# ScalarE's order inside an attention unit: payload rows ahead of the second exponentials, input normalising in two parts

## The chip, the cores and the metric

The kernel runs on one core of one Trainium2 chip. The metric is the device time of one execution in microseconds. The kernel before took 1568.78 us, the median of three runs (1564.93 to 1570.09).

The core's engines run side by side and meet only at semaphores: TensorE (PE in the profile, its weight loads PEld), VectorE (DVE), ScalarE (ACT), GpSimd (POOL) and SyncE (SP, which only issues DMAs here). Each engine works its own list of instructions strictly in the order in which it is written, so a wait at the head of a list holds everything behind it.

## The reference, cut to what matters

`x` is [64, 128, 256], the context `ctx` is [64, 128, 192], and a mask hides some context keys.

```
lat  = layernorm(layernorm(x));  xn = layernorm(ctx) * g + b         # per token
q    = lat @ Wq;  k, v = [xn @ Wkv ; lat @ Wlkv]                     # 4 heads of 64, 256 keys
attn = softmax(rmsnorm(q) * rmsnorm(k) * scale, masked)
x    = x + (attn @ v) @ Wo + bo
n    = layernorm(x)
s    = sigmoid(n @ router) + bias;  best 2 of 4 groups, best 4 of 32 experts, weights w
x    = x + sum_k w_k * expert_k(n) + shared_expert(n)
```

All of it is computed in fp32. The first part, up to the choice of experts, is called the attention stage here. Only that stage is touched by the change.

## The kernel before, in words

**Units.** The 64 batches are worked in 32 units of two batches (j = 0 and 1). A token is a partition, so one batch is one tile of 128 rows. Each engine has a loop `in_order(step, UNITS)`; its `step(s)` handles several units at once: `s` is the unit whose attention is computed, `a = s + 1` is the unit whose queries, keys and values are projected, `s + 2` is the unit whose inputs are normalised and turned, `cc = s - 1` is the unit whose finished rows are normalised again and copied for the experts, and `r = s - 2` is the unit whose rows are ranked and given a place in the experts' lists. Order inside a step is written out by hand for every engine.

**Names and lines that matter below.**

- PE, in its own order: `scores(s,0)` (L676, L680), `project_q`, `project_kv`, `project_v` of `a` (L620, L631/L632, L645), `turn_probs(s,0)` (L689), `project_q(a,1)`, `scores(s,1)`, `project_kv(a,1)`, `mix_values(s,0)` (L701), `turn_probs(s,1)`, `turn_o(s,0)` (L710), `project_v(a,1)`, `turn_k(a,0)` (L657/L658), `mix_values(s,1)` (L701), `positions(r)` (L739 to L743), `turn_n1(cc)` (L607), `out_proj(s,0)` (L719), `turn_o(s,1)` (L710), `turn_k(a,1)`, `logits(cc)` (L728), `turn_q(a)` (L665), `out_proj(s,1)`, `turn_inputs(s+2)` (L590 to L597).
- ACT: `exps` (L996) needs `maxima` of DVE; `projected_kv` (L978, L979, L981) needs `project_kv`; `probs_copy` (L1005) needs `turn_probs`; `o_copy` (L1012) needs `turn_o`; `values_copy` (L988) needs `project_v`; `k_copy` (L1028) needs `turn_k`; `n1_copy` (L1017) needs `turn_n1`. `rows_to_scatter(cc, j)` (L952, one instruction that writes 128x1024 from 128x256) needs DVE's `norms` of this step and an old payload buffer that is free. `normalise(s+2)` needs the same `norms`; it makes `x_hat` (L938, two instructions) and counts `xhat`, then `c_hat` (L943, two instructions) and counts `hats`.
- DVE: `maxima(s,0)` (L1282), the statistics and `norms(s+2)` (ends with L1271), `scale_first(a)` (L1276), `maxima(s,1)` (L1282), `top_scores` and `best_groups` of `r`, `normalise_o(s,0)` (L1290, L1292), `best_experts` and `choose_experts` of `r` (L1344 to L1366; L1362 writes `chosen`), `square_sums(a,1)` (L1242), `scale_second(a)` (nine short links and L1311, which multiplies 128x768 in place), `normalise_o(s,1)` (L1290, L1292), `read_ranks(r)`, `residual(s,0)` (L1302), `assign(r)`, `residual(s,1)`.
- POOL: `add_bias(s+2)` (L507, 128x512 added in place, waits for `hats`), then `places`, `mask_bias(s+2)` (L499, L501), `weights` and the eight indirect DMAs of `scatter(s-2)` (L548), some of which wait for steps of PE so that they are spread over time.
- SP: the loads of a later unit and the blank list pages; a load waits for `hats` and for `mask_ready`, which `mask_bias` counts.

**Waits that tie them.** `mix_values(s,1)` waits for `pt_ev` (both copies of `probs_copy(s,1)`) and for `ot_ev` (`o_copy(s,0)`), because it writes where `turn_o(s,0)` wrote. `turn_n1(cc)` waits for both rows of `rows_to_scatter(cc)`. `turn_o(s,1)` waits for `on_done`, the end of `normalise_o(s,1)`, and in DVE's list that stands behind `scale_second(a)`:

```
pe.wait_ge(pt_ev, b + 1)
pe.wait_ge(pc_free, b + 1)
ge(pe, ot_ev, b)
```

Of the kernel before, what the change touches and what calls it, by code (L numbers as in the profile page):

```python
# [54 lines left out]
def ge(eng, sem, value):  # L55

    if value > 0:
        eng.wait_ge(sem, value)
# [6 lines left out]
def at(start, n):  # L65
    return slice(start, start + n) if isinstance(start, int) else bass.ds(start, n)
# [21 lines left out]
def build(nc, x, ctx, mask, ln_x_g, ln_x_b, ln_l_g, ln_l_b, qn_g, kn_g, wq, wkv, wlkv, wo, bo,  # L88
# [7 lines left out]
    with ExitStack() as c:  # L96
# [203 lines left out]
        def paid(u):  # L300

            if u.n == UNITS - 1:
                return pay_last
            return pay_mid if u.n % 3 == 1 else pay[:, 0:2] if u.n % 3 == 0 else pay[:, 2:4]
# [5 lines left out]
        def scattered(b, units):  # L310

            return 16 * 2 * TOPK * len(range(b, units, 3))
# [618 lines left out]
        def _(act):  # L931
            act.wait_ge(made, MADE)

            def normalise(u):
                act.wait_ge(dN, N_LINKS * (u.n + 1))
                ge(act, t_x, u.n)
                for j in range(2):
                    a = act.activation(x_hat[:, j, :], x1[:, at(2 * u.n + j, 1), :].rearrange("p a n -> p (a n)"),  # L938
                                       ACT.Identity, bias=nb[:, j:j + 1], scale=ra[:, j:j + 1])
                a.then_inc(xhat, 1)  # L940
                ge(act, t_c, u.n)
                for j in range(2):
                    a = act.activation(c_hat[:, j, :], c_in[:, u.par, j, :],  # L943
                                       ACT.Identity, bias=nb[:, 2 + j:3 + j], scale=ra[:, 2 + j:3 + j])
                a.then_inc(hats, 1)

            def rows_to_scatter(u, j):
                if j == 0:
                    act.wait_ge(dN, N_LINKS * (u.n + 4))
                    if u.n != UNITS - 1:  # L950
                        ge(act, scat[u.n % 3], scattered(u.n % 3, u.n))
                act.activation(paid(u)[:, j, :, 0:D], x1[:, at(2 * u.n + j, 1), :].to_broadcast([P, TOPK, D]),  # L952
                               ACT.Identity, bias=nb[:, 4 + j:5 + j], scale=ra[:, 4 + j:5 + j]).then_inc(pay_x, 1)

            def inputs(u):
                act.wait_ge(t_x, u.n + 1)
                ge(act, pc_full, 2 * u.n)
                for k in range(2):
                    a = act.activation(lnT[:, k, :], ps[0][:, k * D:(k + 1) * D], ACT.Identity,  # L959
                                       bias=bl[:, k:k + 1], scale=gl[:, k:k + 1])  # L960
                a.then_inc(e_x, 1)
                act.wait_ge(t_c, u.n + 1)
                act.activation(cT[:, 0, :], ps[1][:, 0:D], ACT.Identity, bias=bx[:, 0:1], scale=gx[:, 0:1])
                act.activation(cT[0:KC, 1, :], ps[1][0:KC, D:2 * D], ACT.Identity,
                               bias=bx[0:KC, 1:2], scale=gx[0:KC, 1:2]).then_inc(e_c, 1)

            def projected_q(u, j):
                b = 2 * u.n + j
                act.wait_ge(pa_full, b + 1)
                ge(act, ss_done, b - 1)  # L970
                act.activation(sq[:, j, 0:2 * D], ps[2][:, :], ACT.Square)
                ge(act, t_q, u.n)
                act.activation(raw[:, j, 0:2 * D], ps[2][:, :], ACT.Copy).then_inc(pa_free, 1)

            def projected_kv(u, j):
                b = 2 * u.n + j
                act.wait_ge(pb_full, b + 1)
                act.activation(sq[:, j, 2 * D:3 * D], ps[3][:, 0:D], ACT.Square).then_inc(sq_full, 1)  # L978
                act.activation(raw[:, j, 2 * D:3 * D], ps[3][:, 0:D], ACT.Copy)  # L979
                ge(act, pv_full, 2 * u.n - 3 + j)  # L980
                act.activation(vv[:, 4 * u.par + 2 * j, :, 0:DH],  # L981
                               ps[3][:, D:2 * D].rearrange("p (h d) -> p h d", d=DH), ACT.Copy).then_inc(pb_free, 1)

            def values_copy(u, j):

                b = 2 * u.n + j
                act.wait_ge(pc_full, b + 1)
                act.activation(vv[:, 4 * u.par + 2 * j + 1, :, 0:DH],  # L988
                               ps[4][:, 0:D].rearrange("p (h d) -> p h d", d=DH), ACT.Copy).then_inc(pc_free, 1)

            def exps(u, j):
                b = 2 * u.n + j
                act.wait_ge(m_done, b + 1)
                ge(act, pt_full, b - 1)
                for g in range(H):
                    a = act.activation(probs[:, j, g, :], psS[:, g // 2, g % 2], ACT.Exp,  # L996
                                       bias=nmax[:, j, g:g + 1])
                a.then_inc(exp_done, 1)

            def probs_copy(u, j):  # L1000
                b = 2 * u.n + j
                act.wait_ge(pt_full, b + 1)
                ge(act, pv_full, b - 1)
                for key in range(2):
                    a = act.activation(probsT[:, j, key, :], psS[:, key].rearrange("p a n -> p (a n)"), ACT.Copy)  # L1005
                a.then_inc(pt_ev, 1)

            def o_copy(u, j):
                b = 2 * u.n + j
                act.wait_ge(ot_full, b + 1)  # L1010
                ge(act, y_full, b)
                act.activation(oT, psO[:, 0:D], ACT.Copy).then_inc(ot_ev, 1)  # L1012

            def n1_copy(u):
                act.wait_ge(t_n, u.n + 1)
                ge(act, lg_full, u.n)
                act.activation(n1T.rearrange("p k n -> p (k n)"), ps[0][:, :], ACT.Copy).then_inc(e_n, 1)  # L1017

            def logit_exp(u):
                act.wait_ge(lg_full, u.n + 1)  # L1020
                ge(act, ch_done, u.n)
                act.activation(esc[:, :, :].rearrange("p j e -> p (j e)"), ps[4][:, D:D + 2 * E], ACT.Exp,
                               scale=-1.0).then_inc(lg_exp, 1)

            def k_copy(u, j):
                act.wait_ge(t_k, 2 * u.n + j + 1)
                ge(act, s_full, 2 * (u.n - 2) + j + 1)
                act.activation(kT[:, 2 * u.par + j].rearrange("p k n -> p (k n)"), ps[1 - j][:, :], ACT.Copy)\  # L1028
                   .then_inc(e_k, 1)

            def q_copy(u):

                act.wait_ge(t_q, u.n + 1)
                act.activation(qT[:, u.par].rearrange("p k j n -> p (k j n)"), ps[1][:, :], ACT.Copy,
                               scale=gqk[:, 0:1]).then_inc(e_q, 1)

            def step(s):
                a, cc = s + 1, s + -1
                if s.exists():
                    exps(s, 0)  # L1040
                if a.exists():
                    projected_q(a, 0)
                    projected_kv(a, 0)
                    values_copy(a, 0)
                if s.exists():
                    probs_copy(s, 0)
                if a.exists():
                    projected_q(a, 1)
                if s.exists():
                    exps(s, 1)  # L1050
                if (s + 2).exists():
                    normalise(s + 2)
                if cc.exists():
                    rows_to_scatter(cc, 0)
                if a.exists():
                    projected_kv(a, 1)
                if s.exists():
                    probs_copy(s, 1)
                    o_copy(s, 0)
                if a.exists():  # L1060
                    values_copy(a, 1)
                if cc.exists():
                    rows_to_scatter(cc, 1)
                if a.exists():
                    k_copy(a, 0)
                if cc.exists():
                    n1_copy(cc)
                if s.exists():
                    o_copy(s, 1)
                if a.exists():  # L1070
                    k_copy(a, 1)
                if cc.exists():
                    logit_exp(cc)
                if a.exists():
                    q_copy(a)
                if (s + 2).exists():
                    inputs(s + 2)

            normalise(Unit(0, 0))
            act.wait_ge(consts, 16 * CONSTS)  # L1080
            inputs(Unit(0, 0))
            for j in range(2):
                projected_q(Unit(0, 0), j)
                projected_kv(Unit(0, 0), j)
                values_copy(Unit(0, 0), j)
            normalise(Unit(0, 1))
            k_copy(Unit(0, 0), 0)
            k_copy(Unit(0, 0), 1)
            act.wait_ge(gains, 2)
# [524 lines left out]
```

## Time and profile before

| | us |
|---|---|
| median of the runs | 1568.78 |
| the profiled execution | 1573.22 |
| its span, first to last instruction | 1571.3 |
| PE busy | 1474.5 (94%) |
| DVE busy | 1131.4 (72%) |
| ACT busy | 992.0 (63%) |
| POOL busy | 642.6 (41%) |

Busy shares are means over the whole program. The attention stage runs from about 30 us to about 890 us; in it DVE is busy more than eight tenths and PE more than nine. A `PE` row and its duration can overlap the next one, since matmuls are pipelined; what shows a stall is the bracket at the end of a row, which gives the idle time before it and the instruction whose end released it. The granted clock of TensorE stands in the columns PEclk: 1.00 is 2.4 GHz and 0.50 is 1.2 GHz. All rows that are read below are of the profiled execution, so sums are made against 1573.22 us.

### The profile page before, as it was taken

How to read it: one execution, taken by the hardware profiler on the slowest of the kernel's cores; microseconds unless marked ns; L12 is line 12 of the kernel's file. 1: busy time of each engine (PE TensorE's matmuls, PEld its weight loads, DVE VectorE, ACT ScalarE, POOL GpSimd, SP SyncE). 2: the span in 40 equal slices, each digit the busy share in tenths (PEclk: the TensorE clock that was granted, in tenths of full speed). 3: DMA queues.
4: the chain of work that ended last, by engine and by line, in shares of the span. 5: the costliest groups of instructions: out<-in, count | busy, mean ns of one | idle time of the engine just before them, and what ended most of it. 6: DMA issues, size and time to landing. Idle time of an engine off the chain costs nothing.

```text
span 1571.3 us, 33151 instructions
## 1 busy us (share of the span) xinstructions
PE 1474.5 (94%) x8902; PEld 1160.9 (74%) x8902; DVE 1131.4 (72%) x4813; ACT 992.0 (63%) x2340; POOL 642.6 (41%) x760
## 2 busy tenths in 40 slices
PE   5999999999999999999999898999999999999997
PEld 2565666666566666656566676999999999997886
DVE  3568888888889888888888774555555555555878
ACT  3666767676677767676676452666666666664332
POOL 2014334343434434343433342666666666661000
PEclk9999999999999999999999799999999999999999
DMA  7122222223222222223240175555555555536886
GB/s 243 40 78 84 106 86 86 108 87 107 87 99 93 95 97 87 105 91 109 84 157 35 49 241 202 167 174 170 175 170 174 171 172 173 164 95 246 295 300 230
DMA packets 118146, 217.28 MB, mean 138 GB/s; under 512 B 19595, under 2 KB 82445, under 8 KB 116688
## 3 DMA queue, kind: packets, MB, share of 16 engines
q1 hardware_dynamic: 91856, 147.75, 29.1%
q0 software_dynamic: 26112, 67.42, 12.2%
q8 instruction: 79, 1.29, 0.3%
q14 instruction: 99, 0.81, 0.2%
HBM read 101.28 MB, written 118.00 MB: 140 GB/s over the span
## 4 chain that ended last, share of the span: by engine, by line
PE 76%; ACT 10%; DVE 8%; issue 5%; SPq 1%; DMA 0%; ACTq 0%; DVEq 0%
PE ps L882 16%; PE psS L892 8%; PE ps L620 8%; PE ps L817 6%; PE psO L701 5%; PE ps L719 4%; PE psS L680 4%; PE ps L873 4%; DVE nmax L1282 2%; PE ps L632 2%; PE psS L676 2%; PE ps L645 2%; ACT arena L996 2%; PE psS L689 2%; PE ps L631 2%
## 5 line engine op out<-in xcount | busy, mean ns | idle before, releaser
L572 POOL DMA_INDIRECT expert_out<-pay,dest x288 | 283.5, 984 | 183.8 <-issue 140.6
L1532 DVE TENSOR_TENSOR history<-history,ps 128x128 f32<-128x128 f32 x288 | 83.0, 288 | 208.1 <-ACT history L1158 208.1
L548 POOL DMA_INDIRECT lists<-pay,slot x168 | 173.6, 1034 | 127.0 <-PE psO L701 53.2
L701 PEld LDWEIGHTS psO<-arena 128*128 128x128 f32 x1024 | 131.7, 208 | 75.4 <-ACT arena L1005 51.2
L701 PE MATMUL psO<-arena 128*128 128x65 f32 x1024 | 140.8, 295 | 44.5 <-ACT arena L1012 44.5
L892 PE MATMUL psS<-arena,history 128*128 x576 | 172.1, 381 | 0.4 <-DVE history L1532 0.4
L996 ACT ACTIVATE arena<-psS,nmax 128x256 f32<-128x256 f32 x256 | 100.4, 475 | 108.2 <-DVE nmax L1282 108.2
L1158 ACT ACTIVATE history<-ps 128x128 f32<-128x128 f32 x288 | 79.9, 278 | 136.5 <-PE ps L882 136.5
L882 PEld LDWEIGHTS ps<-pad 128*128 128x128 f32 x1152 | 151.2, 191 | 9.4 <-ACT pad L1147 2.0
L882 PEld LDWEIGHTS ps<-pad,hist_j 128*128 128x128 f32 x1152 | 151.2, 192 | 7.3
L882 PE MATMUL ps<-pad 128*128 128x128 f32 x1152 | 151.9, 275 | 1.8 <-ACT pad L1152 1.8
L882 PE MATMUL ps<-pad,hist_j 128*128 128x128 f32 x1152 | 151.8, 275 | 0.0
L1539 DVE TENSOR_SCALAR pay<-psS,dest 128x256 f32<-128x256 f32 x288 | 139.4, 484 | 1.4 <-DVE dest L1545 0.8
L620 PE MATMUL ps<-arena 128*128 128x512 f32 x256 | 126.8, 619 | 0.3 <-ACT arena L959 0.3
L548 POOL DMA_INDIRECT lists<-arena,slot x88 | 91.0, 1034 | 62.5 <-PE psO L701 25.3
L1147 ACT ACTIVATE pad<-ps 128x256 f32<-128x256 f32 x288 | 108.0, 375 | 6.0 <-PE ps L873 6.0
L873 PE MATMUL ps<-ident,pay 128*128 128x128 f32 x576 | 109.8, 273 | 0.7 <-issue 0.7
L1282 DVE TENSOR_REDUCE nmax<-psS 128x4 f32<-128x1024 f32 x64 | 78.4, 1225 | 40.3 <-PE psS L680 35.0
L1152 ACT ACTIVATE pad<-arena 128x512 f32 x144 | 89.6, 622 | 0.0
L1152 ACT ACTIVATE hist_j<-arena 128x512 f32 x144 | 89.5, 622 | 0.0
L522 POOL TENSOR_TENSOR pay<-w,wsum 128x8 f32<-128x8 f32 x21 | 4.4, 210 | 205.2 <-DVE arena L1410 205.2
L892 PEld LDWEIGHTS psS<-arena,history 128*128 128x128 f32 x576 | 87.0, 191 | 0.7 <-issue 0.7
(214 smaller groups left out, 3392.0 us busy)
## 6 DMA issues: line engine op xcount, KB each, us to landing
lists<-pad SPq DMA_DIRECT2D x72, 516.0 KB, 4.3
pay<-lists SPq DMA_DIRECT2D x288, 129.0 KB
arena<-expert_out SPq DMA_DIRECT2D x32, 1024.0 KB, 6.8
x<-in_x SPq DMA_DIRECT2D x32, 256.0 KB
out<-arena SPq DMA_DIRECT2D x32, 256.0 KB, 5.7
arena<-in_ctx SPq DMA_DIRECT2D x32, 192.0 KB
expert_out<-pay,dest POOLq DMA_INDIRECT x288
arena<-in_gate SPq DMA_DIRECT2D x2, 2048.0 KB, 16.7
```

Source lines behind the costliest of these rows:

```text
L548: pool.indirect_dma_start(lists, bass.IndirectOffsetOnAxis(ap=slots(u)[:, j, k:k + 1], axis=0), paid(u)[:, j, k, :], None).then_inc(scat[u ...
L572: pool.indirect_dma_start(expert_out, bass.IndirectOffsetOnAxis(ap=dest[:, t % DESTS, 1:2], axis=0), yy[n], None, bounds_check=T * TOPK - ...
L620: m = pe.matmul(ps[2][:, :], lnT[:, k, tok], w_lat[:, k, 0:2 * D], start=k == 0, stop=k == 1)
L701: m = pe.matmul(psO[:, g * (DH + 1):(g + 1) * (DH + 1)], probsT[:, j, key, g * P:(g + 1) * P], vv[:, 4 * u.par + 2 * j + key, h, :], start ...
L873: m = pe.transpose(ps[n % 2][:, k * P:(k + 1) * P], xs[n][:, k * P:(k + 1) * P], ident[:, :])
L882: m = pe.matmul(ps[2 + n % 2][:, which * P:(which + 1) * P], w_now[n % 2][:, k, which * I:(which + 1) * I], xsT[:, n % 2, k * P:(k + 1) * ...
L892: pe.matmul(dbank[n % 2][:, 0:D], hh[:, n % 4, :], w_dn[:, at(e, 1), :].rearrange("p a n -> p (a n)"), start=True, stop=True)\
L996: a = act.activation(probs[:, j, g, :], psS[:, g // 2, g % 2], ACT.Exp, bias=nmax[:, j, g:g + 1])
L1147: act.activation(xsT[:, n % 2, :], ps[n % 2][:, 0:D], ACT.Copy).then_inc(xst_ev, 1)
L1152: act.activation(w_now[n % 2], w_gu[:, at(e, 1)].rearrange("p a k n -> p (a k) n"), ACT.Copy)\
L1282: dve.tensor_reduce(nmax[:, j, :], psS[:, :, :, :].rearrange("p r k n -> p (r k) n"), AX, ALU.max, negate=True).then_inc(m_done, 1)
L1539: dve.tensor_scalar(yy[n], dbank[n % 2][:, 0:D], dest[:, t % DESTS, 0:1].bitcast(fp32), None, ALU.mult)\
```

## The change

`normalise` becomes `normalise_x` (waits for `norms`, makes `x_hat`, counts `xhat`) and `normalise_c` (makes `c_hat`, counts `hats`). In ACT's `step(s)` the order changes; no instruction is added, removed or altered, and no other engine's list is touched.

```
 step, before                      step, after
 ...                               ...
 projected_q(a, 1)                 projected_q(a, 1)
 exps(s, 1)                        rows_to_scatter(cc, 0)
 normalise(s + 2)                  exps(s, 1)
 rows_to_scatter(cc, 0)            projected_kv(a, 1)
 projected_kv(a, 1)                normalise_x(s + 2)
 probs_copy(s, 1)                  probs_copy(s, 1)
 o_copy(s, 0)                      o_copy(s, 0)
 values_copy(a, 1)                 values_copy(a, 1)
 rows_to_scatter(cc, 1)            k_copy(a, 0)
 k_copy(a, 0)                      rows_to_scatter(cc, 1)
                                   normalise_c(s + 2)
 n1_copy(cc)                       n1_copy(cc)
 ...                               ...
```

```diff
-            def normalise(u):
+            def normalise_x(u):
                 act.wait_ge(dN, N_LINKS * (u.n + 1))
                 ge(act, t_x, u.n)
...
                 a.then_inc(xhat, 1)
+
+            def normalise_c(u):
                 ge(act, t_c, u.n)
...
                 if a.exists():
                     projected_q(a, 1)
-                if s.exists():
-                    exps(s, 1)
-                if (s + 2).exists():
-                    normalise(s + 2)
                 if cc.exists():
                     rows_to_scatter(cc, 0)
+                if s.exists():
+                    exps(s, 1)
                 if a.exists():
                     projected_kv(a, 1)
+                if (s + 2).exists():
+                    normalise_x(s + 2)
                 if s.exists():
                     probs_copy(s, 1)
                     o_copy(s, 0)
                 if a.exists():
                     values_copy(a, 1)
+                    k_copy(a, 0)
                 if cc.exists():
                     rows_to_scatter(cc, 1)
-                if a.exists():
-                    k_copy(a, 0)
+                if (s + 2).exists():
+                    normalise_c(s + 2)
```

Ahead of the loop both parts are called one after the other, as `normalise` was.

## Rows read from the trace of the kernel before

**Rows 1.** Windows view of the middle of attention: busy us (instructions) per engine, PEclk, DMA

```profile
82.35:849.54 767.19, 725.65 (x3970) 494.50 (x3971) 655.48 (x3179) 530.39 (x1150) 301.71 (x383) 0.94 0.27 96
```

**Rows 2.** Waits of PE, 82 to 850 us: total us, times, longest

```profile
PE psO L701 <- ACT arena L1012: 43.0, 29, 1.5
```

**Rows 3.** Timeline of PE, end of two units: start, us, work [idle before <-releaser]

```profile
467.16 1.97 PE L701 MATMUL psO<-arena 128*128 128x65 f32 x16 [1.49 <-ACT arena L1012]
...
489.08 1.04 PE L689 MATMUL psS<-ident,arena 128*128 128x128 f32 x8
...
491.51 0.27 PE L658 MATMUL ps<-ident,arena 128*128 128x128 f32 x1
493.26 1.97 PE L701 MATMUL psO<-arena 128*128 128x65 f32 x16 [1.48 <-ACT arena L1012]
...
495.69 1.03 PE L719 MATMUL ps<-arena 128*128 128x256 f32 x4
496.75 0.44 PE L710 MATMUL psO<-ident,arena 128*128 128x128 f32 x2
```

**Rows 4.** Timeline of ACT in the same unit

```profile
486.51 1.57 ACT L996 ACTIVATE arena<-psS,nmax 128x256 f32<-128x256 f32 x4 [1.78 <-DVE nmax L1282]
487.95 1.10 ACT L938 ACTIVATE arena<-x,nb,ra 128x256 f32<-128x256 f32 x2
488.94 0.98 ACT L943 ACTIVATE arena<-arena,nb,ra 128x192 f32<-128x192 f32 x2
489.82 1.24 ACT L952 ACTIVATE pay<-x,nb,ra 128x1024 f32<-128x1024 f32 x1
490.95 0.38 ACT L978 ACTIVATE arena<-ps 128x256 f32<-128x256 f32 x1
...
491.74 1.10 ACT L1005 ACTIVATE arena<-psS 128x512 f32<-128x512 f32 x2
492.70 0.42 ACT L1012 ACTIVATE arena<-psO 128x256 f32<-128x256 f32 x1
```

**Rows 5.** Timeline of DVE in the same unit

```profile
483.45 0.16 DVE L1271 SCALAR_TENSOR_TENSOR nb<-mv,ra 128x6 f32<-128x6 f32 x1
...
485.25 1.23 DVE L1282 TENSOR_REDUCE nmax<-psS 128x4 f32<-128x1024 f32 x1 [0.65 <-PE psS L680]
...
491.01 0.87 DVE L1362 TENSOR_TENSOR chosen<-r,t 128x64 bf16<-128x64 f32 x1
...
495.18 0.96 DVE L1311 TENSOR_TENSOR arena<-arena,rq 128x768 f32<-128x768 f32 x1
```

**Rows 6.** Timeline of PE, a unit with the clock falling behind it

```profile
438.05 2.74 PE L701 MATMUL psO<-arena 128*128 128x65 f32 x16 [1.48 <-ACT arena L1012]
```

**Rows 7.** Windows view, PE alone: busy us (instructions), PEclk, DMA share, GB/s

```profile
439.10:445.80 6.70, 6.70 (x35) 0.50 0.62 229
...
878.60:882.00 3.40, 3.40 (x24) 1.00 0.00 0
```

**Rows 8.** Timeline of DVE in unit 30, where `s + 2` doesn't exist

```profile
867.65 1.22 DVE L1282 TENSOR_REDUCE nmax<-psS 128x4 f32<-128x1024 f32 x1 [0.50 <-PE psS L680]
...
876.94 0.96 DVE L1311 TENSOR_TENSOR arena<-arena,rq 128x768 f32<-128x768 f32 x1
```

**Rows 9.** Timeline of PE in unit 30

```profile
878.51 0.44 PE L710 MATMUL psO<-ident,arena 128*128 128x128 f32 x2 [0.98 <-DVE arena L1292]
```

**Rows 10.** Timeline of POOL: the bias addition in three places

```profile
32.61 1.96 POOL L507 TENSOR_TENSOR x<-x,bo_b 128x512 f32<-128x512 f32 x1 [12.01 <-ACT arena L943]
...
55.66 1.28 POOL L507 TENSOR_TENSOR x<-x,bo_b 128x512 f32<-128x512 f32 x1 [21.09 <-ACT arena L943]
...
490.50 1.28 POOL L507 TENSOR_TENSOR x<-x,bo_b 128x512 f32<-128x512 f32 x1
```

**Rows 11.** Timeline of ACT and DVE beside the first two of them

```profile
32.49 0.96 DVE L1311 TENSOR_TENSOR arena<-arena,rq 128x768 f32<-128x768 f32 x1
...
54.59 0.99 ACT L943 ACTIVATE arena<-arena,nb,ra 128x192 f32<-128x192 f32 x2
```

More of the change, by code:

```diff
@@ L1048, in step @@
                     projected_q(a, 1)
+                if cc.exists():
+                    rows_to_scatter(cc, 0)
                 if s.exists():
                     exps(s, 1)
-                if (s + 2).exists():
-                    normalise(s + 2)
-                if cc.exists():
-                    rows_to_scatter(cc, 0)
                 if a.exists():
                     projected_kv(a, 1)
+                if (s + 2).exists():
+                    normalise_x(s + 2)
                 if s.exists():
@@ L1077, in step @@
                     inputs(s + 2)
-            normalise(Unit(0, 0))
+            normalise_x(Unit(0, 0))
+            normalise_c(Unit(0, 0))
             act.wait_ge(consts, 16 * CONSTS)
@@ L1085, in _ @@
                 values_copy(Unit(0, 0), j)
-            normalise(Unit(0, 1))
+            normalise_x(Unit(0, 1))
+            normalise_c(Unit(0, 1))
             k_copy(Unit(0, 0), 0)
```

## The prediction, made before the changed kernel ran

> **What bounds the kernel now.** I read the 40 slices first: attention fills more than half of the span, and behind the first slice PE is busy for nine tenths or eight, DVE is close behind, and ACT has room. So ACT's order matters only where ACT is the last to release PE. The view of waits says where that is: PE waits in one place, the second `mix_values` (L701), 29 times, 43.0 us in all, each time released by `o_copy` (L1012) [rows 2]. The timeline of PE shows the place: `turn_k(a,0)` ends at 491.51 + 0.27 = 491.78, and the mixing starts at 493.26 after 1.48 us of nothing [rows 3]. The timeline of ACT says why: between the second exponentials (486.51) and `probs_copy` (491.74) stand 1.87 us of normalising (487.95 to 489.82), 1.13 us of payload rows (489.82 to 490.95) and 0.79 us of projected copies [rows 4]. ACT had stood still for 1.78 us just ahead of those exponentials.
>
> The stall has a second price. From 82.35 to 849.54 us there are 28 unit periods (29 stalls) in 767.19 us: 27.40 us each, at a mean granted clock of 0.94 [rows 1]. But the period from 467.16 to 493.26, in which the clock stayed full, took 26.10 us [rows 3]. So 767.19 - 28 x 26.10 = 36.4 us are spent on a lower clock; a stretch of it is seen right behind the stall that ended at 438.05: 0.50, that is 1.2 instead of 2.4 GHz, from 439.10 to 445.80 [rows 6, 7].
>
> **The change, part by part.** Times are those of the unit that ends with the row at 496.75.
>
> *First payload rows ahead of the exponentials.* They need `norms`, which ends with L1271 at 483.45 + 0.16 = 483.61 [rows 5], and ACT, free at 486.51 - 1.78 = 484.73 [rows 4]. They end at 484.73 + 1.24 = 485.97, 0.54 us ahead of the exponentials' release. DVE always makes `norms` before `maxima(s,1)`, so the new wait can't hold the exponentials. Cost nothing, cover 1.78 us; without the cover it would be at most 1.24 us per unit.
>
> *Projected copies, then `normalise_x`.* The copies start at 487.95 instead of 490.95 and end after 0.79 at 488.74; `normalise_x` (0.99, 487.95 to 488.94) ends at 489.73 [rows 4]. `probs_copy` then waits for `turn_probs`, 489.08 + 1.04 = 490.12 [rows 3]: 0.39 us to spare.
>
> *`probs_copy` and `o_copy`.* Started at 490.15, `probs_copy` gives way to `o_copy` after 0.96, at 491.11, which ends after 0.42 at 491.53 [rows 4]. That is ahead of 491.78. The mixing follows `turn_k` directly, at about 491.62 by the spacing of 0.11 between such rows. The 1.48 us go.
>
> *Second rows and `normalise_c` behind `k_copy`.* `k_copy` can start at 491.82 and holds ACT for some 0.48 (half of `probs_copy`'s 0.96); the rows start at 492.30 and end at 493.54. `turn_n1` needs them after the mixing and `positions`, at about 493.6: even, within 0.1 us, and what follows covers that. `normalise_c` runs from 493.43 to 494.42. `hats` is then 494.42 instead of 489.92: 4.5 us late. `norms` and `turn_inputs` want it in the next unit or at the end of this one, over 5 us later: nothing. `add_bias` on POOL moves from 490.50 to 494.50 (it started 0.08 after `hats` at 55.66, against 54.59 + 0.99 [rows 10, 11]), and behind it `places`, `mask_bias` and, through `mask_ready`, SP's loads and blank pages. SP's list holds only loads and pages for later units; scatter of this unit waits for `assign` anyway. I take 0 for these; the nearest bound is the 4.0 us shift itself, against a need more than a unit away.
>
> *What is late next: DVE.* `turn_o(s,1)` started at 496.75, a moment behind the L719 rows at 495.69 [rows 3]. With PE 1.64 us earlier (493.26 to 491.62) it would be ready at about 495.1, but it waits for `normalise_o(s,1)`, behind `scale_second` on DVE. Unit 30 of this same trace shows the new arrangement, since it has no `s + 2` and so no normalising: no stall at the mixing, and 0.98 us of idleness at `turn_o`, released by DVE [rows 9]. From `maxima(s,1)` to L1311 it is 876.94 - 867.65 = 9.29 us there [rows 8], against 495.18 - 485.25 = 9.93 now [rows 5]. The 0.64 us are those that L1362 loses: it starts at 491.01 and ends at 491.88, just behind the bias addition on POOL, 490.50 + 1.28 = 491.78 [rows 5, 10]. That addition moves away from it. So on a full clock the period becomes 26.10 - 0.64 = 25.46 us, not 26.10 - 1.48.
>
> *Clock.* Behind the 0.98 us of unit 30 the clock stayed at 1.00 [rows 7], where behind 1.48 us it fell in most units. I take it that the 36.4 us come back whole; the other bound is that none do.
>
> **Sum.** 29 x 0.64 = 18.6, and 36.4: 55 us. Against the profiled execution, 1573.2 - 55 = 1518.2 us. The median of the runs is 4.4 us below that execution; since part of that spread may be the clock's, which would be gone, I take off half: **1516 us**.
>
> **Rivals.**
>
> *A. POOL takes DVE's operand.* One mechanism, and it decides the sign. The bias addition would start at 494.50; L1311, which reads two operands from SBUF, at 485.25 + 9.29 = 494.54. The trace has both orders of such a pair: L1362 waited out POOL's addition; and at 32.61 the addition took 1.96 instead of 1.28 us because L1311 had begun at 32.49 [rows 10, 11]. If POOL is first, L1311 goes on only at 494.50 + 1.28 = 495.78 and ends 0.10 + 0.96 - 0.12 later, 496.62, against 494.54 + 0.96 = 495.50: 1.12 us late (with 0.12 of its 0.96 done before it needs the operand, as L1362's rows suggest). It lies on the path to `turn_o`. The period is 25.46 + 1.12 = 26.58, PE's idleness there 0.98 + 1.12 = 2.10 us, longer than 1.48, and the clock falls after it: at 36.4 / 28 = 1.30 us a unit the period is 27.88 against 27.40, +14 us, **1587 us** on the profile's time. With falls in half the units it is 27.23, -5 us: 1568, no change. It decides at which of the two starts first, and 0.04 us is less than my chain is sure of. For it: every start is tied to PE, so the race repeats alike in each unit. Against it: each 0.05 us that ACT is later than I have it gives DVE the race, where POOL's wait costs nothing.
>
> The Trainium skill has the rule behind this race ("SBUF — State Buffer", section "Who interferes with whom"): a VectorE instruction with two SBUF inputs contends with a GpSimd instruction that reads SBUF, and whichever issues first keeps the shared pair for its whole length. This case's rows agree in both orders. By that rule the change is worth what the race gives: 1518 or 1587.
>
> *B. The race is mixed*, unit by unit. Half the units at 25.46 and half at 26.58 plus 1.30: mean 26.67, so 29 x 0.73 = 21 us: 1552 us; with fewer falls 1535. Middle 1544.
>
> *C. The clock still falls behind 0.98 us.* Then only 29 x 0.64 = 18.6 us come: 1555 us. Unit 30 speaks against it, but it is one unit.
>
> *D. The edit moves no release*, because ACT isn't what PE waits for. The view of waits names L1012 29 times, and unit 30 loses the stall with the normalising; I give it next to nothing.
>
> **How the numbers follow.** Forecast (DVE first, clock full) 0.42; A 0.26, of which 0.16 slower and 0.10 near the time before (a part of that a little faster); B 0.20; C 0.12. A measurement of this kernel can tell 0.3%, 4.7 us. Faster: 0.42 + 0.20 + 0.12 + 0.02 = 0.76; the same 0.08; slower 0.16. The range starts at 1507 (all of the 4.4 us off, and some 7 us if the unstalled units also lose their 0.1 us gaps) and goes up through C, B and the near half of A to 1574, leaving out the slower 0.16.
>
> **What the profile after would show.** Right: L1012 is gone from PE's waits at L701; L710 waits for L1292, about 0.98 us, 29 times; L952 stands ahead of L996, whose idle time falls from 1.78 to about 0.54; L1362 takes a quarter of its 0.87 us; L1311 starts 9.29 us after L1282; periods near 25.46 and a granted clock near 1.00. Wrong by A: L1311 takes about 2.1 us beside L507, L710 waits 2 us, PEclk stays near 0.94. Wrong by C: the same waits as the forecast, but PEclk at 0.94. A wait of L607 for L952 would say that the second rows come too late, one of L996 for `norms` that the first do.

## The result, and the profile after

The changed kernel takes **1624.97 us** (median of 4 runs, 1608.89 to 1627.14) where the kernel before took 1568.59 on the same chip (1564.93 to 1570.09): a ratio of 1.034 (95% interval 1.027 to 1.041). It is slower, outside the range of 1507 to 1574 us, and it went the way of rival A. The profiled execution took 1622.99 us, its span 1621.1 against 1571.3, so 49.8 us are to be found. Ratios below are of fast runs; one run, the 1661.06 us of experiment 2, was a slow one and counts only in that experiment's median. The lines of POOL and PE keep their numbers; those of ACT and DVE move by 2 to 5 (L952 becomes L954, L996 L998, L1012 L1014, L1282 L1287, L1292 L1297, L1311 L1316, L1362 L1367).

First the page of the kernel after: its engines, and the granted clock in 40 slices.

```profile
PE 1508.6 (93%) x8902; PEld 1183.9 (73%) x8902; DVE 1139.7 (70%) x4813; ACT 995.7 (61%) x2340; POOL 661.4 (41%) x760
...
PEclk9999899888988998989989989999999999999999
```

The windows view of the stretch of [rows 1], with the same columns:

```profile
82.35:849.54 767.19, 713.68 (x3714) 486.07 (x3714) 622.05 (x2991) 497.57 (x1070) 298.45 (x359) 0.90 0.25 89
```

Less work of every engine fits into the same 767.19 us, and the clock is 0.90 where it was 0.94. The waits of PE from 82 to 905 us are one row, to be laid beside [rows 2]:

```profile
PE psO L710 <- DVE arena L1297: 57.6, 28, 2.1
```

The wait for `o_copy` is gone, and a longer one, for DVE, stands in its place. The timeline of PE shows a unit and the next one's end, as [rows 3] and [rows 9] do:

```profile
485.42 0.27 PE L658 MATMUL ps<-ident,arena 128*128 128x128 f32 x1
485.58 1.97 PE L701 MATMUL psO<-arena 128*128 128x65 f32 x16
...
488.01 1.03 PE L719 MATMUL ps<-arena 128*128 128x256 f32 x4
491.10 0.49 PE L710 MATMUL psO<-ident,arena 128*128 128x128 f32 x2 [2.06 <-DVE arena L1297]
...
520.96 0.44 PE L710 MATMUL psO<-ident,arena 128*128 128x128 f32 x2 [2.06 <-DVE arena L1297]
```

The second mixing follows `turn_k(a,0)` at once; `turn_o(s,1)` comes 2.06 us late, and this period took 520.96 - 491.10 = 29.86 us. Behind it the clock is at 1.2 GHz (windows view, PE alone):

```profile
491.40:498.10 6.70, 6.70 (x30) 0.50 0.60 226
```

Why DVE is late shows in its timeline and POOL's, the pair that rival A set against each other [rows 5, 10]:

```profile
488.45 2.04 DVE L1316 TENSOR_TENSOR arena<-arena,rq 128x768 f32<-128x768 f32 x1
490.41 0.17 DVE L1295 RECIPROCAL rden<-psO 128x4 f32<-128x4 f32 x1
490.62 0.42 DVE L1297 TENSOR_TENSOR arena<-psO,rden 128x256 f32<-128x256 f32 x1
```

```profile
488.42 1.26 POOL L507 TENSOR_TENSOR x<-x,bo_b 128x512 f32<-128x512 f32 x1 [4.03 <-ACT arena L945]
...
518.28 1.26 POOL L507 TENSOR_TENSOR x<-x,bo_b 128x512 f32<-128x512 f32 x1 [4.02 <-ACT arena L945]
```

POOL's bias addition starts 0.03 us ahead of DVE's product, and the product takes 2.04 us instead of the 0.96 of [rows 5]. The view by source line says that this isn't one unit: minimum, median and maximum of L1316 are

```profile
L1316 DVE TENSOR_TENSOR arena<-arena,rq x32: 957/2041/2055, 31.4 to 928.0; 128x768 f32<-128x768 f32 x32
```

**Where the 49.8 us are.** From the L710 row at 107.91 to the one at 900.81 us there are 27 periods:

```profile
107.91 0.44 PE L710 MATMUL psO<-ident,arena 128*128 128x128 f32 x2 [2.05 <-DVE arena L1297]
...
900.81 0.60 PE L710 MATMUL psO<-ident,arena 128*128 128x128 f32 x2 [2.06 <-DVE arena L1297]
```

That is 29.37 us each, against 27.40 before [rows 1]: 27 x 1.97 = 53 us. By the starts of DVE's product the first units give 5.9 us back (the fourth stands at 105.26 against 111.14), and the last period costs 4.4 us more (29.87 against 25.47), which leaves under 2 us for all the rest. Why the first units are shorter isn't shown. The 27 periods aren't alike: 11 take 28.2 us, 13 take 29.9 and 3 take 31.4.

### The profile page after: what moved, and what is told of

Same layout as the page of the kernel before. It is cut to its first block, busy times and chain, and to the rows that moved or that the text cites. A ratio compares the mean times of both kernels' runs of the same rounds, so it can differ in the third digit from the quotient of the medians.

```text
span 1621.1 us, 33151 instructions
## 1 busy us (share of the span) xinstructions
PE 1508.6 (93%) x8902; PEld 1183.9 (73%) x8902; DVE 1139.7 (70%) x4813; ACT 995.7 (61%) x2340; POOL 661.4 (41%) x760
## 3 DMA queue, kind: packets, MB, share of 16 engines
q1 hardware_dynamic: 91856, 147.75, 28.2%
## 4 chain that ended last, share of the span: by engine, by line
PE 71%; DVE 21%; issue 5%; ACT 1%; DMA 1%; SPq 1%; ACTq 0%; DVEq 0%
PE ps L882 16%; PE psS L892 8%; PE ps L620 7%; PE ps L817 5%; PE psS L680 4%; PE ps L873 4%; PE ps L719 3%; PE ps L728 3%; PE ps L632 2%; PE psS L676 2%; PE ps L645 2%; DVE nmax L1287 2%; PE psS L689 2%; PE ps L631 2%; DVE ss L1247 2%
## 5 line engine op out<-in xcount | busy, mean ns | idle before, releaser
L1287 DVE TENSOR_REDUCE nmax<-psS 128x4 f32<-128x1024 f32 x64 | 78.4, 1224 | 105.3 <-PE psS L680 101.1
L998 ACT ACTIVATE arena<-psS,nmax 128x256 f32<-128x256 f32 x256 | 100.4, 475 | 83.5 <-DVE nmax L1287 83.5
L701 PEld LDWEIGHTS psO<-arena 128*128 128x128 f32 x1024 | 120.8, 194 | 28.6 <-issue 24.5
L701 PE MATMUL psO<-arena 128*128 128x65 f32 x1024 | 128.8, 279 | 1.3 <-ACT arena L1014 1.3
L507 POOL TENSOR_TENSOR x<-x,bo_b 128x512 f32<-128x512 f32 x32 | 41.2, 1288 | 187.5 <-ACT arena L945 187.4
L719 PE MATMUL ps<-arena 128*128 128x256 f32 x256 | 91.0, 493 | 0.0
```

Of the source, the lines that this page charges most:

```text
L701: m = pe.matmul(psO[:, g * (DH + 1):(g + 1) * (DH + 1)], probsT[:, j, key, g * P:(g + 1) * P], vv[:, 4 * u.par + 2 * j + key, h, :], start ...
L719: m = pe.matmul(ps[2 + j][:, 0:D], oT[:, k * P:(k + 1) * P], w_o[:, k, :], start=k == 0, stop=k == 1)
L1287: dve.tensor_reduce(nmax[:, j, :], psS[:, :, :, :].rearrange("p r k n -> p (r k) n"), AX, ALU.max, negate=True).then_inc(m_done, 1)
```

## The experiments

The question is what made 1.97 us a unit: the lost race, the lower clock, or both, and whether the rest of the change does what the prediction said. The theories in the expectations: **P**, the lost race lengthens DVE's product and the clock falls behind the longer wait; **L**, the late hats themselves (`normalise_c` and all behind it) cost the time; **C**, the clock falls behind any wait at `turn_o`. Added lines shift the later numbers by a few, so L710 may stand as L711 or L712. Each experiment has the kernel before beside it on its own chip: 1661.33 us in experiments 1 to 4, 1569.11 in 5, 6, 7 and 10, and 1645.15 in 8, 9 and 11. Periods in attention agree between the chips to a few hundredths of a microsecond; so ratios are compared, and times only within a chip.

### 1. The bias addition behind the product

```diff
                 ge(pool, hats, u.n + 1)
+                ge(pool, scaled[1], upto(u.n, UNITS))
                 xu = x1[:, at(2 * u.n, 2), :]
```

> The changed kernel, with one wait more on POOL: the bias addition of a unit waits until DVE's scale_second (L1316) of that step is done, so the two never overlap. Theory P (the operand race: POOL's addition starts 0.03 us ahead of L1316 and holds it for 1.1 us, and the longer idleness of PE brings the lower clock): L1316 is back at 0.96 us, PE's wait at the second turn_o falls from 2.06 to 0.98 us, the clock stays full in attention, a unit takes 25.46 us, and the whole about 1518 us. Rival L (it is not the race but the lateness of hats: POOL's and SP's work comes 4 to 5 us later and disturbs the rest): POOL is later still here, so no better than the changed kernel, 1620 us or more. Rival C (the clock falls behind 0.98 us of idleness too): 25.46 us plus 1.3 us a unit, about 1555 us.

Measured: 1611.78 against 1661.33 us, ratio 0.970 (0.965 to 0.975), 49.6 us faster than before. POOL's and DVE's timelines and the waits of PE from 100 to 800 us:

```profile
437.91 1.27 POOL L508 TENSOR_TENSOR x<-x,bo_b 128x512 f32<-128x512 f32 x1 [5.21 <-DVE arena L1317]
```

```profile
436.80 0.96 DVE L1317 TENSOR_TENSOR arena<-arena,rq 128x768 f32<-128x768 f32 x1
```

```profile
PE psO L711 <- DVE arena L1298: 28.6, 30, 1.0
```

One wait on one engine turns the change from 3% slower into 3% faster. The product takes 0.96 us again, PE waits about 1 us a unit, and the period is 463.86 - 438.37 = 25.49:

```profile
438.37 0.44 PE L711 MATMUL psO<-ident,arena 128*128 128x128 f32 x2 [0.99 <-DVE arena L1298]
...
463.86 0.44 PE L711 MATMUL psO<-ident,arena 128*128 128x128 f32 x2 [0.97 <-DVE arena L1298]
```

The hats are as late as in the kernel after and the addition later still, so L falls. The clock stays at 1.00 in the windows view, so C falls too:

```profile
82.35:800.00 717.65, 689.01 (x3995) 459.58 (x3995) 647.28 (x3201) 531.57 (x1151) 301.14 (x385) 1.00 0.28 103
```

### 2. POOL delayed by one small instruction

```diff
                 ge(pool, hats, u.n + 1)
+                pool.memset(spacer[:, u.n:u.n + 1], 0.0)
                 xu = x1[:, at(2 * u.n, 2), :]
```

> The changed kernel, with one tiny instruction on POOL (a memset of 128x1) between the wait for hats and the bias addition, so that the addition starts 0.05 to 0.2 us later and just loses the race with L1316. Theory P: if the delay is over 0.03 us plus what the two engines differ in reaching their operand, L1316 takes 0.96 us in most units, the addition takes some 2 us instead, and the time is that of e1, about 1518 us; a mixture of 0.96 and 2.04 would say that the race is decided within hundredths. Rival L: lateness is the same as in the changed kernel, so 1620 us. Rival C: about 1555 us.

Measured: 1639.21 us, ratio 0.983 (0.979 to 0.988): between the two outcomes. The shift was of some hundredths, and both starts now fall together. Two units in a row, POOL and then DVE:

```profile
426.48 2.09 POOL L509 TENSOR_TENSOR x<-x,bo_b 128x512 f32<-128x512 f32 x1
...
451.95 1.26 POOL L509 TENSOR_TENSOR x<-x,bo_b 128x512 f32<-128x512 f32 x1
```

```profile
426.48 0.96 DVE L1318 TENSOR_TENSOR arena<-arena,rq 128x768 f32<-128x768 f32 x1
...
451.96 2.07 DVE L1318 TENSOR_TENSOR arena<-arena,rq 128x768 f32<-128x768 f32 x1
...
478.54 0.96 DVE L1318 TENSOR_TENSOR arena<-arena,rq 128x768 f32<-128x768 f32 x1
```

At 426.48 DVE wins and POOL's addition takes 2.09; at 451.95 POOL wins and DVE's product takes 2.07. POOL wins in 10 of 28 units. This is rival B of the prediction made to order. PE's timeline has both waits:

```profile
454.63 0.44 PE L712 MATMUL psO<-ident,arena 128*128 128x128 f32 x2 [2.10 <-DVE arena L1299]
...
480.10 0.44 PE L712 MATMUL psO<-ident,arena 128*128 128x128 f32 x2 [0.98 <-DVE arena L1299]
```

The clock didn't fall behind that wait of 2.10 us (windows view, PE alone), and from this product to the next it is 478.54 - 451.96 = 26.58 us. So it went in 2 of the 10 lost units; the 8 with a lower clock behind the wait take 28.2 to 31.4 us, and most of the won ones 25.47.

```profile
454.60:480.10 25.50, 24.49 (x142) 1.00 0.28 102
```

### 3. The first half of the change alone

```diff
                     projected_q(a, 1)
+                if cc.exists():
+                    rows_to_scatter(cc, 0)
                 if s.exists():
...
                     normalise(s + 2)
-                if cc.exists():
-                    rows_to_scatter(cc, 0)
```

> One part of the change alone, on the kernel before: the first payload rows go ahead of the second exponentials, and normalise stays whole and where it was. POOL's addition keeps its old place (beside L1362). The wait at the second mixing falls from 1.48 to about 0.35 us, and PE meets the rest at turn_o, since DVE ends no earlier: about 1.1 us there; a unit on a full clock stays at 26.10 us. Theory P with the clock's share: two short waits bring fewer falls than one of 1.48 us; with none left it is 1573 - 36 = 1537 us. If the clock falls as often as before: no change, 1573 us. Rival L says nothing is late here, so the best part of the change's gain should show: about 1518 us.

Measured: 1630.03 us, ratio 0.981 (0.977 to 0.984). PE's waits from 100 to 800 us:

```profile
PE psO L710 <- DVE arena L1292: 32.0, 28, 2.3
PE psO L701 <- ACT arena L1012: 9.5, 27, 0.5
```

In a unit these are 1.15 and 0.35 us, together about the 1.48 of [rows 3], and the full-clock period of 26.12 is that of before. But the clock is 1.00 in all but one place:

```profile
82.35:800.00 717.65, 675.69 (x3868) 447.19 (x3867) 639.90 (x3122) 516.97 (x1121) 294.47 (x373) 1.00 0.28 99
```

So this half won its 1.9% by the clock alone: in this kernel the same waiting in two pieces made the clock fall once and not in most units.

### 4. The second half of the change alone

The diff is against the kernel after. `normalise_x` and the first rows stand behind the exponentials, in the order of the kernel before; `normalise_c` stays behind the copies, and `k_copy` ahead of the second rows.

```diff
-                if cc.exists():
-                    rows_to_scatter(cc, 0)
                 if s.exists():
                     exps(s, 1)
-                if a.exists():
-                    projected_kv(a, 1)
                 if (s + 2).exists():
                     normalise_x(s + 2)
+                if cc.exists():
+                    rows_to_scatter(cc, 0)
+                if a.exists():
+                    projected_kv(a, 1)
```

> The other part of the change alone: normalise_c moves behind the copies and k_copy goes ahead of the second rows, but exponentials, normalise_x and the first rows keep their old order. hats is late as in the changed kernel, and some 0.2 us later still, since probs_copy and o_copy end later. The bias addition would start about 0.2 us behind L1316. Theory P: DVE wins the race, L1316 takes 0.96 us, PE waits about 0.6 us at the second mixing and about 0.4 us at turn_o, a unit takes 25.46 us on a full clock, and the whole about 1518 us. Rival L: hats is later than in the changed kernel, so 1620 us or more. Rival C: about 1555 us.

Measured: 1608.34 us, ratio 0.967 (0.963 to 0.971), 53 us faster than before. ACT is later by enough that POOL starts second:

```profile
461.57 0.96 DVE L1316 TENSOR_TENSOR arena<-arena,rq 128x768 f32<-128x768 f32 x1
```

```profile
462.12 1.54 POOL L507 TENSOR_TENSOR x<-x,bo_b 128x512 f32<-128x512 f32 x1 [4.61 <-ACT arena L945]
```

```profile
433.95 1.97 PE L701 MATMUL psO<-arena 128*128 128x65 f32 x16 [0.61 <-ACT arena L1014]
437.66 0.44 PE L710 MATMUL psO<-ident,arena 128*128 128x128 f32 x2 [0.26 <-DVE arena L1297]
...
463.14 0.44 PE L710 MATMUL psO<-ident,arena 128*128 128x128 f32 x2 [0.25 <-DVE arena L1297]
```

The period is 463.14 - 437.66 = 25.48. A mixing that waits 0.61 us for ACT again costs nothing here: as long as DVE's chain is whole, it sets the period. So each half of the change alone makes the kernel faster, by 1.9% and 3.3%, and both together make it 3.4% slower: only together do they put the two starts 0.03 us apart.

### 5. The changed kernel again

> The changed kernel itself once more, so that it stands beside the others on one chip. Both theories: the ratio to the kernel before is near the 1.034 measured, and L1316 takes 2.04 us in every unit.

Measured: 1612.01 (1608.22 to 1625.76) against 1569.11 us, ratio 1.027 (1.024 to 1.030). The idle time at L710 is 2.04 to 2.06 us in each of 28 units, as in the first trace; the race isn't a matter of luck.

### 6. PE kept busy through the whole wait

```diff
+            def keep_busy(u):
+                for n in range(BUSY):
+                    pe.matmul(psS[:, 0, 0, 0:P], ident[:, :], ident[:, :], start=True, stop=True)
...
                     out_proj(s, 0)
+                    keep_busy(s)
                     turn_o(s, 1)
```

with BUSY = 17: work without a use, to hold the clock while the wait stays.

> The changed kernel with 17 matmuls of 128x128 more on PE between out_proj(s,0) and turn_o(s,1), into a part of psS that nobody reads; at 0.11 us each they fill 1.87 of the 2.06 us of waiting, and change nothing else. It separates the two prices of the lost race. Theory P: the race is lost as before (L1316 2.04 us), but the clock stays full in attention, so a unit takes 26.6 us where the changed kernel takes 28.2 or 29.9: against the kernel before (27.40) that is 0.8 us less a unit, a ratio of about 0.985. If the clock has no part in it, the period stays at 28 to 30 us and the ratio at 1.034. If the clock falls for a reason other than PE's idleness, the same.

Measured: 1595.7 us, ratio 1.017 (1.014 to 1.020); a miss in size. One such matmul takes 0.22 us, not the 0.11 that I had read from the transposes, so 17 take 3.74 us and overran the wait. The clock was full throughout, and the period 28.07 us (472.53 - 444.46 by the rows of the second mixing), still less than the 29.37 of the kernel after.

### 7. The kernel before, with the wait of experiment 1

> The kernel before, with the wait of e1 on POOL: its bias addition no longer meets L1362, so DVE is 0.64 us earlier, but ACT's order is the old one and PE still waits 1.48 us at the second mixing. Theory P: PE is ready for turn_o only at about 496.6 in the unit shown, 0.15 us before it started, so at most 0.15 us a unit comes: ratio 0.995 to 1.000. If DVE alone had bounded the unit: 0.64 us a unit, ratio 0.988.

The edit is that of experiment 1, in the kernel before. Measured: 1568.52 us, ratio 0.999 (0.997 to 1.001).

```profile
PE psO L702 <- ACT arena L1013: 38.2, 26, 1.5
```

The addition off L1362's path shortens DVE's chain, but PE still waits 1.5 us for ACT. By the starts of DVE's product a unit whose clock didn't fall takes 25.86 us instead of 26.11, one with a fall 27.46 in both kernels. So the 0.64 us of DVE is worth next to nothing without ACT's new order.

### 8. PE kept busy for the length of the wait

As experiment 6, with BUSY = 8.

> As e6_fill_the_wait, with 8 matmuls more on PE instead of 17. There each turned out to take 0.22 us, not 0.11: 17 took 3.74 us, and turn_o(s,1) started about 1.57 us after its operand was there (period 28.07 us, and no lower clock anywhere in attention). Eight take 1.76 of the 2.06 us of waiting. Theory P: clock full, L1316 still 2.04 us, a period of 26.6 us, ratio to the kernel before about 0.985. If the lost race alone made the changed kernel slower: ratio above 1.00.

Measured: 1620.27 against 1645.15 us, ratio 0.985 (0.983 to 0.988).

```profile
454.53 0.44 PE L711 MATMUL psO<-ident,arena 128*128 128x128 f32 x2 [0.28 <-DVE arena L1303]
...
481.10 0.44 PE L711 MATMUL psO<-ident,arena 128*128 128x128 f32 x2 [0.28 <-DVE arena L1303]
```

```profile
82.35:800.00 717.65, 710.02 (x4273) 493.44 (x4272) 642.19 (x3070) 514.89 (x1107) 308.64 (x369) 1.00 0.28 101
```

This is the run that separates the two prices. DVE loses the race in each of 28 units as in the kernel after (its product takes 2.05 us), `turn_o(s,1)` is as late, but the clock is 1.00: the period is 26.57 us. The 26.58 us of experiment 2, a lost race without a fall and without a filler, say the same. With its race lost and its clock whole the change would be 1.5% **faster** than before; what makes it slower is the clock.

### 9. The bias addition in two instructions

```diff
-                xu = x1[:, at(2 * u.n, 2), :]
-                pool.tensor_tensor(xu, xu, bo_b[:, :].rearrange("p (o n) -> p o n", o=1).to_broadcast([P, 2, D]),
-                                   ALU.add).then_inc(biased, 1)
+                for j in range(2):
+                    xu = x1[:, at(2 * u.n + j, 1), :].rearrange("p a n -> p (a n)")
+                    m = pool.tensor_tensor(xu, xu, bo_b[:, :], ALU.add)
+                m.then_inc(biased, 1)
```

> The changed kernel with POOL's bias addition as two instructions of 128x256 instead of one of 128x512. If the first to start holds the operand for its whole instruction, L1316 gets it between the halves: about 1.4 us instead of 2.04, and PE waits about 1.4 us at turn_o, a period of 25.9 us on a full clock. The clock decides the rest: with a fall in most units as in the kernel before (1.5 us of waiting there) 27.3 us, no change; with few, 0.975. If L1316 stays at 2.0 us (POOL keeps the operand over both): as the changed kernel, 1.03.

Measured: 1620.21 us, ratio 0.985 (0.983 to 0.988).

```profile
421.59 1.51 DVE L1317 TENSOR_TENSOR arena<-arena,rq 128x768 f32<-128x768 f32 x1
```

```profile
421.56 2.12 POOL L508 TENSOR_TENSOR x<-x,bo_b 128x256 f32<-128x256 f32 x2 [4.16 <-ACT arena L946]
```

POOL is first by the same 0.03 us, but DVE waits out only the first half: 1.51 us instead of 2.04. The hold lasts as long as the one instruction. PE waits 1.52 us, and the clock falls in 8 of 28 units.

### 10. and 11. Two tries at a better version

The first takes experiment 1, puts DVE's `normalise_o(s,1)` ahead of the 128x768 product, and lets PE do `logits(cc)` ahead of `turn_k(a,1)`:

```diff
+                ge(pool, scaled[1], upto(u.n, UNITS))
...
-                if a.exists():
-                    turn_k(a, 1)
                 if cc.exists():
                     logits(cc)
+                if a.exists():
+                    turn_k(a, 1)
...
                     normalise_o(s, 1)
+                if a.exists():
+                    multiply_second(a)
```

> Meant to beat all: e1, and on DVE normalise_o(s,1) goes ahead of the 128x768 product of scale_second (L1316 of the changed kernel), and on PE logits(cc) goes ahead of turn_k(a,1), which wants that product. turn_o(s,1) should find its operand ready (0.98 us of idleness gone), and logits cover most of the 0.5 us by which the product is later. Expected: PE without waits over 0.2 us in a unit, a period of 24.5 to 24.9 us, which is PE's own work (26.10 - 1.48 = 24.6), against 25.5 of e1: another 20 us, ratio about 0.957 against 0.970 of e1. If DVE, whose own work is about 24.5 us too, becomes the bound: 25.0 to 25.3 us.

Measured: 1517.83 against 1569.11 us, ratio 0.969 (0.965 to 0.972): a miss, no better than 1 or 4, with a period of 25.66. `turn_o` waits no more, but `logits` does, 0.8 us a unit from 100 to 800 us ("issue": the profile shows no releaser), and DVE's ranks go slower beside the moved addition:

```profile
PE ps L729 <- issue: 23.4, 28, 0.8
```

```profile
413.44 1.26 POOL L508 TENSOR_TENSOR x<-x,bo_b 128x512 f32<-128x512 f32 x1 [5.70 <-DVE arena L1319]
```

```profile
414.03 0.71 DVE L1397 TENSOR_SCALAR need<-need_i 128x32 int32<-128x32 int32 x1
```

The 0.71 us are 0.17 in the kernel after. DVE is busy for 646 of the 700 us from 100 to 800, and the addition met another of its instructions: the collision was only moved. The second try keeps the first one's order on PE, and puts the product behind `read_ranks` and the addition on POOL behind the weights, where DVE works on statistics:

```diff
-                ge(pool, scaled[1], upto(u.n, UNITS))
+                ge(pool, y_done, 2 * (u.n - 1))
...
                 if r.exists():
                     read_ranks(r)
+                if a.exists():
+                    multiply_second(a)
```

> e8_best took 25.66 us a unit with DVE busy throughout; in it L508 overlapped DVE's assign and cost it some 0.9 us, and logits waited for read_ranks. Here read_ranks goes ahead of the 128x768 product, and POOL adds the bias only after residual(s,1), when DVE runs maxima and the statistics, which read one operand each; scatter comes behind it. Expected: DVE without lengthened instructions, 24.7 to 25.0 us a unit, and a ratio of 0.950 to 0.956. If something else bounds it (scatter late, PE), 25.5 us or more.

Measured: 1613.84 against 1645.15 us, ratio 0.982 (0.979 to 0.984); a miss, with most periods between 26.3 and 26.7. DVE's maxima now wait 43.8 us in all, 24 times, for a scores signal that reaches it some 1.7 us behind the last scores matmul:

```profile
DVE nmax L1289 <- remote: 43.8, 24, 1.9
```

Why the signal is late stays open; no run here tells.

## Why the prediction was wrong, point by point

**Right, and confirmed alone.**

- The first rows ahead of the exponentials cost nothing: ACT's idle time there went from 1.78 to 0.65 us [rows 4], and the exponentials' release is still DVE's:

```profile
478.53 1.24 ACT L954 ACTIVATE pay<-x,nb,ra 128x1024 f32<-128x1024 f32 x1
480.42 1.57 ACT L998 ACTIVATE arena<-psS,nmax 128x256 f32<-128x256 f32 x4 [0.65 <-DVE nmax L1287]
...
485.04 0.39 ACT L1014 ACTIVATE arena<-psO 128x256 f32<-128x256 f32 x1
```

- The 1.48 us at the second mixing go. `o_copy` ends at 485.04 + 0.39 = 485.43, in time for the mixing at 485.58.
- L1362 loses its 0.64 us (L1367 takes 0.23), and the product starts 9.29 us behind the maxima (488.45 - 479.16), to the hundredth as forecast. Rows of DVE in the kernel after:

```profile
479.16 1.23 DVE L1287 TENSOR_REDUCE nmax<-psS 128x4 f32<-128x1024 f32 x1 [0.65 <-PE psS L680]
...
484.92 0.23 DVE L1367 TENSOR_TENSOR chosen<-r,t 128x64 bf16<-128x64 f32 x1
```

- With the race won, the period of 25.46 and the 0.98 us at `turn_o` are those of experiment 1 (25.49, 0.97 to 0.99), the clock stays full, and the forecast 55 us are 49.6 there and 53 in experiment 4. So rival C is out, and the sum was right for the branch that it was made for.
- Rival A's 1.12 us, its 2.10 us of idleness and its full-clock period of 26.58 are 1.08 (2.04 - 0.96), 2.06 and, in experiment 8, 26.57.

**The step that failed** is "It decides at which of the two starts first, and 0.04 us is less than my chain is sure of", read as 0.42 for DVE and 0.26 for POOL. My own chain had POOL at 494.50 and DVE at 494.54, POOL first; measured, POOL is first by 0.02 to 0.04 us in all 28 settled units. I then leaned on "each 0.05 us that ACT is later than I have it gives DVE the race", without a row that said ACT would be later. The honest reading of that chain was A first. What the runs showed in its place: POOL first, the product at 2.04 us instead of 0.96, and a wait of 2.06 us at `turn_o` with the lower clock behind it.

The sum for A also has a slip. "Ends 0.10 + 0.96 - 0.12 later, 496.62" leaves the 0.10 out of its result; with it the sum is 496.72, and 1.22 us late. Measured, the product ends 490.49 - 489.68 = 0.81 us behind the addition, so the result without the 0.10 is the near one.

**The term that was mis-sized** is the clock's in rival A: "at 36.4 / 28 = 1.30 us a unit" gave 1587 us. Measured it is 29.37 - 26.57 = 2.80 us a unit. The split of the 1.97 us is then:

| | before | after | difference | x 27 |
|---|---|---|---|---|
| period at full clock | 26.10 | 26.57 | 0.47 | 13 us |
| lower clock | 1.30 | 2.80 | 1.50 | 40 us |
| period | 27.40 | 29.37 | 1.97 | 53 us |

The term grew for three reasons. First, 1.30 us is a mean over 28 units, and the clock fell in only 23 of them: a unit with a fall paid 36.4 / 23 = 1.58 us. After, it falls in all 28, and 26.58 + 1.58 = 28.16 us is what the shortest periods, 28.2, measure. Second, in the longer periods PE spends more time at 1.2 GHz: a mean of 0.90 instead of 0.94 over 767.19 us is 2 x 0.10 x 767 = 153 us at the lower level, against 92 (the means are rounded, so give or take 8 us). Third, more of it counts: PE at half speed can lose at most half of that, 77 us after and 46 before; after, 767.19 / 29.37 = 26.1 units lose 26.1 x 2.80 = 73 us, before it was 36.4. In the unit shown 6.70 us at 0.50 cost 29.86 - 26.57 = 3.29 us, the half of it, 3.35, almost whole. That the rest in the kernel before was hidden under its waits for ACT and DVE is argued, not tested. Carrying over the 1.30 was wrong because the wait of 2.06 us isn't the wait of 1.48. Why the lower clock also lasts longer behind it isn't shown. Nor does the length of the wait alone decide: 1.52 us at L710 brought a fall in 8 of 28 units (experiment 9), and 1.48 us at L701 in 23 of 29. The 2.80 us are those of the two traces, too: the runs of the kernel after with a mean granted clock of 0.935 to 0.938, both traced ones among them, took 1623 to 1627 us, and those with 0.944 to 0.947 took 1608 to 1613.

The Trainium skill's rule ("SBUF — State Buffer", section "Who interferes with whom"), that the one of the pair that issues first keeps the shared pair of ports for its whole instruction, held in both orders: experiment 2 has DVE at 0.96 beside POOL at 2.09, and POOL at 1.26 beside DVE at 2.07, and experiment 9 shows that the length is that of one instruction.

## What to carry to other kernels

When a moved step lands beside an instruction that it can collide with, work out both starts. If the chain says they are a few hundredths apart, take the order that it gives, price both outcomes, and put a wait or a longer step between them; here one wait was worth some 6%. A new wait on TensorE must be priced with the clock behind it, and not by the mean price of another wait: behind 1 us in one piece the clock stayed full here, behind 2 us it cost 2.8 us more a unit.

## What the runs showed of the hardware that was not expected

- **The race repeats.** POOL ahead by 0.02 to 0.04 us wins in each of 28 units, in the result, in experiments 5 and 6, and in experiment 8 on another chip; only with starts within 0.01 us of each other do both orders occur (experiment 2).
- **The same waiting counts otherwise in one piece than in two.** The clock fell behind 1.48 us at L701 in 23 of 29 units, behind 0.35 + 1.15 us once (experiment 3), behind 0.98 us in none from 100 to 800 us (experiment 1), behind 1.52 us in 8 of 28 (experiment 9), behind 2.06 us in all 28, and behind 2.10 us in 8 of 10 (experiment 2).
- **A plain 128x128 fp32 matmul takes twice a transpose of that size**, 0.22 against 0.11 us (experiment 6), and each leaves two records, a transpose one: 8 show as x16 in the timeline of experiment 8, where 425.73 + 1.95 is its whole stretch.

```profile
425.73 1.95 PE L716 MATMUL psS<-ident 128*128 128x128 f32 x16
```

- **The expert stage differs from chip to chip.** The kernel before took 1661.33 us on one and 1569.11 on another, 5.9% more, with attention alike. In the windows view of 300 us of the expert stage PE gets through 2216 instructions in the kernel after on the chip of the result (the kernel before takes 1568.59 us there), and through 1932 in experiment 1 on the slower one, at nearly the same granted clock. What sets it stays open; no kernel here was made for it.

```profile
1000.00:1300.00 300.00, 296.58 (x2216) 283.44 (x2217) 153.60 (x552) 194.27 (x542) 175.91 (x180) 0.98 0.57 169
```

```profile
1000.00:1300.00 300.00, 264.31 (x1932) 241.44 (x1933) 128.89 (x483) 171.25 (x485) 158.45 (x161) 0.99 0.48 143
```
